# One sequential kernel, re-timed by hand: expert work two slots earlier, and stages re-filled on five queues

## What is computed

```
for each of 16 chunks of 128 tokens, four heads:
    out   = (silu(q W0^T) * (q W2^T)) W1^T            # with the weights so far
    dW    = gradients from k, v with those weights     # dW0, dW1, dW2
    M     = dW + mean(momentum) * M
    X     = M / |M|;  5 times:  A = X X^T;  B = b A + c A A;  X = a X + B X
    W     = renorm(W + X)                              # used by the next chunk
attention: windows of 128 + 128 keys, softmax, 2 heads of 128
y      = x + (norm(out) * scale + attention) Wo
experts: scores = sigmoid(xn gate^T); 2 of 4 groups of 8 experts, then 8 experts a token
         h = relu(x_lat w1_e)^2 * weight;  routed = sum_e(h w2_e) fc2
shared : relu(xn up)^2 down                            # 512 wide
result = y + routed + shared
```

## Time and profile before

| | us |
|---|---|
| median of 3 runs | 764.44 (762.72 to 765.95) |
| the profiled execution | 764.44 |
| its span, first to last instruction | 762.5 |
| PE busy | 662.8 (87% of the span) |
| DVE busy | 545.3 (72%) |
| ACT busy | 408.4 (54%) |
| POOL busy | 235.5 (31%) |

### The profile page before, as it was taken

How to read it: one execution, slowest core, us unless ns; L and a number is a source line. 1 busy time by engine, 2 the same in 40 slices (tenths; PEclk the granted TensorE clock), 3 DMA queues, 4 the chain that set the end, 5 groups by cost and what they waited for, 6 DMA issues and landing times.

```text
span 762.5 us, 22396 instructions
## 1 busy us (share of the span) xinstructions
PE 662.8 (87%) x8887; PEld 549.6 (72%) x8887; DVE 545.3 (72%) x1893; ACT 408.4 (54%) x1061; POOL 235.5 (31%) x299
## 2 busy tenths in 40 slices
PE   4788787999998889999999999999999999996865
PEld 2667565777786677878788788877878778784654
DVE  6865887685564496777868778687777867758673
ACT  3576352543543547656465564755657476462541
POOL 2422122146762131312213131132221313117761
PEclk9799989999999899999999999999999999999997
DMA  8300000041102024453552545444454544101221
GB/s 276 123 2 2 1 3 1 2 174 38 46 20 78 30 63 141 135 181 120 155 180 93 182 129 172 154 140 161 130 178 140 159 135 142 36 5 32 61 80 52
DMA packets 40152, 75.38 MB, mean 99 GB/s; under 512 B 9712, under 2 KB 24432, under 8 KB 40048
## 3 DMA queue, kind: packets, MB, share of 16 engines
q1 hardware_dynamic: 36224, 68.08, 28.0%
q0 software_dynamic: 2048, 4.33, 1.9%
q10 hardware_dynamic: 1776, 1.54, 0.6%
HBM read 64.73 MB, written 9.20 MB: 97 GB/s over the span
## 4 chain that ended last, share of the span: by engine, by line
PE 52%; DVE 28%; ACT 7%; issue 7%; POOL 3%; DMA 2%; SPq 0%; DVEq 0%; ACTq 0%; POOLq 0%
PE CC L828 16%; PE YB L828 12%; PE HB L828 10%; PE M L828 8%; DVE hb L1698 4%; DVE Am L1408 2%; POOL xsrc L447 2%; ACT hb L562 2%; DVE Mp L1414 2%; PE CC L921 1%; ACT XT L562 1%; DVE comb L1517 1%; PE M L1010 1%; PE CC L960 1%; POOL r L422 1%
## 5 line engine op out<-in xcount | busy, mean ns | idle before, releaser
L422 POOL TENSOR_TENSOR r<-r,half 128x3 f32<-128x3 f32 (+1 forms) x78 | 88.6, 1142 | 206.8 <-DVE r L1285 112.9
L1408 DVE TENSOR_TENSOR Am<-CC,shifts 128x192 f32<-128x192 f32 x150 | 47.6, 352 | 80.9 <-PE CC L828 80.7
L562 ACT ACTIVATE XT<-CC 128x256 f32<-128x256 f32 x150 | 50.9, 382 | 85.0 <-PE CC L922 84.6
L828 PE MATMUL YB<-e_s,hb 128*128 128x128 f32 x560 | 78.3, 283 | 5.9 <-DVE hb L1698 5.9
L562 ACT ACTIVATE hb<-HB 128x512 f32<-128x512 f32 x86 | 51.3, 597 | 54.6 <-PE HB L828 53.4
L828 PE MATMUL HB<-xsT,e_s 128*128 128x128 f32 x560 | 78.8, 284 | 1.7 <-issue 1.7
L828 PEld LDWEIGHTS YB<-e_s,hb 128*128 128x128 f32 x560 | 68.6, 191 | 16.1 <-DVE hb L1698 9.5
L1698 DVE TENSOR_TENSOR hb<-hb,cwb 128x512 f32<-128x512 f32 x70 | 76.1, 1087 | 0.0
L828 PEld LDWEIGHTS HB<-xsT,e_s 128*128 128x128 f32 x560 | 68.3, 192 | 4.6 <-issue 1.8
L828 PE MATMUL CC<-X,Mp 64*64 64x64 f32 x1800 | 57.0, 234 | 16.5 <-DVE Mp L1414 16.5
L828 PE MATMUL CC<-Am 64*64 64x64 f32 x1800 | 55.9, 233 | 14.0 <-DVE Am L1408 13.9
(11 more groups left out here) (229 smaller groups left out, 1505.9 us busy)
## 6 DMA issues: line engine op xcount, KB each, us to landing
e_s<-in_e1T SPq DMA_DIRECT2D x35, 512.0 KB, 4.6
e_s<-in_e2T SPq DMA_DIRECT2D x35, 512.0 KB, 5.6
cwb<-tile_weights SPq DMA_DIRECT2D x35, 512.0 KB, 3.7
sorted_rows<-e_s SPq DMA_DIRECT2D x5, 476.0 KB, 10.2
xs<-sorted_rows SPq DMA_DIRECT2D x35, 68.0 KB, 5.3
sorted_out<-yo SPq DMA_DIRECT2D x35, 64.0 KB, 2.9
out<-xnT_all SPq DMA_DIRECT2D x8, 256.0 KB, 2.1
x_all<-in_x SPq DMA_DIRECT2D x1, 1408.0 KB, 14.8
```

The source lines that it names most:

```text
L422: return pool.tensor_tensor(dst, src, expo[:, 0:n], ALU.pow)
L562: return nc.scalar.activation(out_, in_, func, **kw)
L828: return pe.matmul(out_, lhsT, rhs, start=start, stop=stop)
L1408: nc.vector.tensor_tensor(Am[g][:, :, :], PROD[g], shifts[:, it, :].unsqueeze(1).to_broadcast([P, 3, HD]), ALU.add)\
```

## The change

Five things are altered; no instruction's shape is, and nothing is computed otherwise.

1. The tables: routed units start at slot 35, where it was 37, and the shared units move with them by two or three slots.
2. The routing steps on DVE: one after each group's part of each stage (in step 1 only after group 1), where they stood after three of four stages in ones, twos and threes. PE's `prefixes` stands at stage 11, before at 14.
3. POOL's transfers: 3, 4, 5, 5, 3 behind the five places, before 4, 5, 6, 6, 3; scatters start in step 2 behind "key norm" (before: behind "row norm"), gathers in step 13 behind "output norm" (before: "row norm").
4. In each step: unit 3's second product and its first product change places (PE stages 5 and 6, before 7 and 5); on ACT relu and square of it stand at 6 and 7; on DVE `h_weight(3)` at 9 (before 7), `att_out` at 17 (before 18), `h_weight(5)` at 18 (before: in the tail, ahead of `renorm`); on PE `h_slot(7)` stands ahead of both `turn_w`, before between them.
5. The last two steps: the sixth pair's `last_sum`, `last_turn`, `last_yT`, `last_fc2` go into step 14's tail, ahead of `turn_w`, and in the closing step the rest stand elsewhere.

```diff
-FIRST = 4 * PER + 5
-SHARED = [2 * PER + 1, 2 * PER + 2, 2 * PER + 3, 2 * PER + 5, 2 * PER + 6, 2 * PER + 7,
-          3 * PER, 3 * PER + 1, 3 * PER + 3, 3 * PER + 4, 3 * PER + 6, 3 * PER + 7, 4 * PER, 4 * PER + 1,
-          13 * PER + 3, 13 * PER + 5]
+FIRST = 4 * PER + 3
+SHARED = [PER + 6, PER + 7, 2 * PER, 2 * PER + 1, 2 * PER + 3, 2 * PER + 4, 2 * PER + 5, 2 * PER + 7,
+          3 * PER, 3 * PER + 2, 3 * PER + 3, 3 * PER + 5, 3 * PER + 6, 4 * PER, 13 * PER + 1, 13 * PER + 3]
...
-                move(i, "key side", 4)
+                move(i, "key side", 3)
...
-            SCATTER_AT, GATHER_AT = (2, 4), (13, 4)
+            SCATTER_AT, GATHER_AT = (2, 3), (13, 2)
...
-                        4: [lambda: prep_qk(m)], 5: [lambda: prep_v(m), lambda: h_slot(i, 3)],
-                        7: [lambda: prep_small(m), lambda: y_slot(i, 3)],
+                        4: [lambda: prep_qk(m)], 5: [lambda: prep_v(m), lambda: y_slot(i, 3)], 6: [lambda: h_first(i, 3)],
+                        7: [lambda: prep_small(m), lambda: h_sq(i, 3)],
...
                 if i == LAST - 1:
                     last_yT(4)
+                    last_yT(5)
...
                     att_turn(i)
-                    last_turn(5)
                     q_out(i)
-                    last_fc2(5)
                     att_scores(i, True)
                     last_turn(6)
+                    last_fc2(6)
                     att_turn_p(i, True)
-                    last_fc2(6)
                     att_pv(i)
                     last_turn(7)
+                    last_fc2(7)
                     turn_comb(i)
-                    last_fc2(7)
                     out_wo(i)
...
-                        5: [lambda: h_slot(i, 3)], 7: [lambda: y_slot(i, 3)], 8: [lambda: prep_mom(m)],
+                        5: [lambda: y_slot(i, 3)], 6: [lambda: h_slot(i, 3)], 8: [lambda: prep_mom(m)],
...
                 y_slot(i, 7)
+                h_slot(i, 7)
+                if i == LAST - 1:
+                    last_turn(5)
+                    last_fc2(5)
                 turn_w(m, 0)
-                h_slot(i, 7)
                 turn_w(m, 1)
...
-                        7: [lambda: prep_silu_v(m), lambda: h_weight(i, 3)], 8: [lambda: prep_ss8(m), lambda: shared_add(i, 3)],
-                        9: [lambda: prep_mean(m)],
+                        7: [lambda: prep_silu_v(m)], 8: [lambda: prep_ss8(m)],
+                        9: [lambda: h_weight(i, 3), lambda: prep_mean(m)],
...
-                        18: [lambda: att_out(i)]}
+                        17: [lambda: att_out(i)], 18: [lambda: h_weight(i, 5)]}
...
+                        if routing and (i, st) >= (SORT_STEP, 1) and (g or i > SORT_STEP):
+                            routing.pop(0)()
...
-                    if st % 4 != 1 and (i, st) > (SORT_STEP, 1):
-                        for n in range(1 if i == SORT_STEP else 3 if st % 4 == 3 else 2):
-                            if routing:
-                                routing.pop(0)()
...
-                h_weight(i, 5)
                 renorm(m)
                 w_bd(m)
+                if i == LAST - 1:
+                    last_sum(5)
+                    last_out(4)
                 total(i)
```

More of the change, by code:

```diff
@@ L501, in body @@
                     rms_pow(i)
+                    while moved:
+                        moved.pop(0)()
                     return
@@ L506, in body @@
                 k_u(i, 1)
-                move(i, "key side", 4)
+                move(i, "key side", 3)
                 for g in range(G):
                     ss_pow(i, g)
-                move(i, "momentum norm", 5)
-                fill = {3: [lambda: rms_pow(i), lambda: move(i, "output norm", 6)],
-                        9: [lambda: prep_n8(m), lambda: move(i, "key norm", 6)],
+                move(i, "momentum norm", 4)
+                fill = {3: [lambda: rms_pow(i), lambda: move(i, "output norm", 5)],
+                        9: [lambda: prep_n8(m), lambda: move(i, "key norm", 5)],
                         16: [lambda: window(m)], 17: [lambda: prep_kl(m)]}
@@ L522, in body @@
                     row_pow(m, g)
-                move(i, "row norm", 2 * NT if i == LAST - 1 else 3)
+                move(i, "row norm", 3)
             def move(i, behind, count):
@@ L736, in body @@
                     gate_sig(i)
-                    last_yT(5)
+                    q_out(i)
                     act.preload_act_table_set("natural_log_exp_and_others")
-                    q_out(i)
                     last_yT(6)
@@ L1165, in body @@
                 if i == SORT_STEP:
-                    fill[14] = [prefixes] + fill[14]
+                    fill[11] = [prefixes] + fill[11]
                 if i == LAST - 1:
@@ L1735, in body @@
                     q_ms(i)
-                    last_out(5)
                     att_mask(i)
                     att_max(i)
-                    q_norm(i)
                     last_sum(7)
                     last_out(6)
+                    q_norm(i)
                     att_out(i)
@@ L1751, in body @@
                 grad(i)
-                shared_add(i, 0)
                 sum_copy(i, 0)
@@ L1756, in body @@
                 x_first(i)
+                shared_add(i, 0)
                 fill = {0: [lambda: shared_add(i, 1), lambda: att_scale(i)], 2: [lambda: h_weight(i, 1), lambda: shared_add(i, 2)],
                         3: [lambda: q_ms(i)], 5: [lambda: q_norm(i), lambda: prep_silu_qk(m)],
-                        6: [lambda: h_weight(i, 2), lambda: prep_z(m)],
-                        7: [lambda: prep_silu_v(m), lambda: h_weight(i, 3)], 8: [lambda: prep_ss8(m), lambda: shared_add(i, 3)],
-                        9: [lambda: prep_mean(m)],
+                        6: [lambda: h_weight(i, 2), lambda: prep_z(m), lambda: shared_add(i, 3)],
+                        7: [lambda: prep_silu_v(m)], 8: [lambda: prep_ss8(m)],
+                        9: [lambda: h_weight(i, 3), lambda: prep_mean(m)],
                         10: [lambda: lr_a(m), lambda: prep_qkn(m), lambda: shared_add(i, 4)],
@@ L1797, in body @@
                 if i == LAST - 1:
-                    last_out(4)
-                    last_sum(5)
+                    last_out(5)
             dve.wait_ge(e_init, 2)
```

## The result

The changed kernel took **770.09** in the median (767.25 to 771.63), the kernel before, timed beside it, 765.61: ratio **1.006**, interval 1.0046 to 1.0075. It is slower. The forecast of 761.7 was wrong in sign; the time lies above the range. A few executions ran in a far slower state (one of the kernel before took 1494.83), and all ratios here, and the median of experiment 5, leave them out.

The account below looks back on a forecast made before the run. It took PE, busy 87% of the span, and the waits between engines in one chain of steps as the bound. Its terms by step summed to -2.7 from 764.44, giving 761.7, range 755.2 to 769.0.

Parts of the forecast that it names:

- Step 2: Second step: step 3's old pattern plus a second product, the tail and scatters make it 53.5, +2.2 (0 to +4).
- Step 3: Third step: 4.0 less fill at 0.64 a microsecond, plus 0.6 for the tail and stages: -2.0 (-3.4 to -0.5).
- Step 4: Fourth step: waits and half-clock stretches go because other work holds those places; 46.9, -7.0 (-8 to -3).
- step 1: First step after step 0: routing between Am and Mp and two shared units lengthen it by 3.0 (+1 to +5).
- Steps 5 to 12: The eight steady steps: +0.6 each from the step's end and stages 5 to 9, +4.8 (-2 to +13).
- stages 5 to 9: Within steps 5 to 12: unit 3's new order covers PE's wait but delays X and XT; +0.2 a step (-0.3 to +0.5).
- the prediction's sentence by the rule: End of steps 5 to 12: comb ends 0.28 after the first or second kl, tail about +0.1 or +0.7.
- Step 13: Thirteenth step: 4.5 less fill gives -1.8, `att_out` +0.4, together -1.4.
- closing step: Last stretch: DVE's 3.49 wait goes, `turn_w` 2.2 later, att_pv up to 1.9 earlier less 0.4; -1.5 (-3 to +1).
- Neutral steps: Rival: steps 5 to 12 stay at 46.5, steps 1 to 4 and 13 lose 0.3 less each; 755.4, chance 0.25.
- The clock: Rival: in step 4 TensorE's lower clock or late rows keep 3.5 of the 7.0; 765.2, chance 0.17.
- Slower: Rival: comb waits for all POOL's kl and vl, 0.9 more a step in steps 2 to 13; 772.5, chance 0.13.

Follow-up runs that it names:

- experiment 5: The changed kernel with `att_out` back at stage 18 and `h_weight(5)` back in the tail ahead of `renorm`: median 767.1, ratio 1.0009 to the kernel before.
- experiment 1: The changed kernel with `shared_add(i, 0)` put back ahead of `sum_copy`: 766.9, ratio 0.9998 to the kernel before.
- experiment 2: The kernel before with only `shared_add(i, 0)` moved behind `x_first`: 771.25, ratio 1.0059 to the kernel before.
- experiment 4: The changed kernel with step 2's routing and scatters in the old rhythm and POOL's transfers in the old numbers: 768.89, ratio 1.0034 to the kernel before.
- run 9: Run 8 with the sixth pair's work and the closing step's order also put back, gathers staying early: 761.05, ratio 0.9917 to the kernel before.
- run 8: The changed kernel with `shared_add(i, 0)` back ahead of `sum_copy` and `h_slot(7)` back between the turns of W: 762.55, ratio 0.9937 to the kernel before.
- 11: Run 9 with `last_fc2(6)` moved ahead of `att_turn_p` in the closing step: 760.45, ratio 0.9942 to the kernel before.

## Why the prediction was wrong, point by point

**Step 2, the step that failed.** The prediction gave step 2 "step 3's old pattern plus a second product" and took step 3's length for it. It read the table of slots and not where DVE's `shared_add(i, 0)` had gone, past `x_first`; the prediction has no sentence on that move. It held step 3's pattern to be unchanged when the instruction that had let it run without a wait was moved in the same diff. The wait and the slow clock behind it are 4.0 in the profile and 4.8 by the ratios (experiment 1); the same move alone costs the kernel before 4.5 (experiment 2). The remaining 54.54 is 1.0 over the forecast 53.5, in the upper half of its bounds. Which term this 1.0 belongs to is open: for routing and scatters the prediction had +1.0, and undoing both gave back 0.6 (experiment 4). The other moved one, `shared_add(i, 3)`, was not tried in these steps.

**Step 3, -2.0 against +1.3.** Two mistakes. First, the boundary: in step 2 the time from the end of the last Mp to the end of `renorm` fell from 6.75 to 5.24, but from that Mp to the end of the next momentum it is 14.69 before and 14.93 after. So what step 2 seems to save at its end, step 3 pays at its start (its momentum ends at +9.69, before at +7.94); that PE's queue of shared products is the bound there is argued, not shown. Second, the fill: behind the momentum step 3 is only 0.4 shorter for two products less. Two products left its start (the first Am came 1.7 sooner after the momentum) and one left the second iteration (-1.6); the third changed by -0.7; but one came into the first iteration, which had none (+1.75), and one into the last, which had one (+1.7). Over steps 1 to 4 the forecast had -3.8. In run 9, which has neither the wait nor the new order of turns, they take 200.5, in the kernel before 200.4: what step 4 gives, steps 1 to 3 take. The fill of these four is 66.0 after and 61.5 before, for which 0.64 a microsecond would ask +2.9; the half-clock stretches that step 4 had before are in the same sum, so it neither bears the 0.64 out nor refutes it.

**Step 4 and step 1** came out as forecast: 46.5 where no half-clock stretch fell in (46.9 forecast), 47.85 with one; step 1 +2.7 for +3.0. That step 1 agrees to 0.3 is luck in part, for it took 46.95 to 49.05 in the profiles with the new table and 43.4 to 44.7 in those with the old. The reason for step 4, PE idling in a step with no excuse, was right too. The fault was to count it as a net gain of the table.

**Steps 5 to 12**, mis-sized by 4.0 in all. The parts, a step each: `att_out` +0.24 (forecast +1.0), `h_weight(5)` -0.39 and the order of the turns +0.34 (together forecast -0.6), stages 5 to 9 -0.12 (forecast +0.2). They sum to +0.07; measured +0.08 in most steps. For `att_out` comb's time was the smaller part: 0.57 and not 0.82. The larger was the update's start, which the prediction put at "some 0.8 later"; it had been held by comb before. For the turns the sign was wrong: the prediction named the lost cover of ACT's copies and then gave the reordering a gain. Comb ran from 456.04 to 456.61, beside the pair of kl's. The first kl took 0.62 and ended at 456.33, 0.28 before comb; the second took 0.80 and ended at 457.09. So comb waited for one kl and held up the other, as the prediction's sentence by the rule had it, and not for all three products. The Trainium skill ("SBUF — State Buffer", section "Who interferes with whom") states that such a pair of instructions contends for an exclusive lock; the trace agrees.

**Steps 13, 14 and closing.** Step 13 was as long as before, with 4.5 less fill (46.65 and 46.71). The -1.8 for it was too much by the prediction's own rows: 1.8 is what step 1 saves by having none of the 18.0. Whether the fill was worth nothing or the gathers that now start in step 13 (POOL busy 21.17 against 11.00) took it back was not tested. In the closing step DVE's wait of 3.49 went, as forecast, and `turn_w` came 3.2 after the second Wn against 1.1 before: 2.1, where 2.2 were forecast. The loss behind att_pv, put at 0.4, was 1.8, since `last_fc2(7)` ran at 1.2 GHz ahead of comb's turn.

**The rivals.** "Neutral steps" was right for steps 5 to 12, and only partly by its own reasons: comb was let in after the first kl and stages 5 to 9 gained, but the loss by the turns and the gain by `h_weight(5)`, 0.34 and 0.39, it did not name. "The clock" held 1.3 of step 4. "Slower" gave the sign by a mechanism that did not occur: comb never waited for all of POOL's products. The prediction would have called itself wrong if the steady steps moved by more than 1; they moved by 0.08, and it was wrong by a step that it counted once.

## What to carry to other kernels

When a diff changes a table and moves an instruction, run the new table through the new order: find every place where two users of one buffer follow each other, and ask what frees it between them. Fill that is moved is paid where it lands; only the waits that it covers are won. Undo the parts of a many-part change one at a time: here two parts won 0.34 percent by themselves, undoing two others took 1.2 percent off the changed kernel (from 1.006 to 0.9937), and the sum hid both.

## What the runs showed of the hardware

- DVE's hb (two inputs in SBUF) and POOL's vl, both times recorded 0.02 apart with vl first, took 1.08 and 1.58 in the changed kernel, and 1.55 and 0.61 in run 8. Step 11 of the changed kernel has it the other way as well, 1.54 and 0.61. One of the two runs at its own speed (1.07 and 0.61 where nothing is beside) and the other's time grows by 0.97 or 0.48; which one it is, the recorded starts don't tell.
- Each PE wait of 2.00 to 2.06 ahead of a shared product, in all seven profiles that have one, was followed by a granted clock of 1.2 GHz (from 133.1 in the changed kernel, from 183.2 and 237.9 in experiment 2), and the product took 2.6 to 3.6; in experiment 1, without the wait, the clock stayed and it took 1.89.
- The profiled last two steps of runs 9 and 11 differ by 5.4 (71.1 and 65.7) at one moved instruction; before the closing step their code is the same, and step 14 alone differs by 2.7, with TensorE at half clock for 6.8 from 700.5 in the one and not at all in the other. The medians differ by 0.6. A single profile can't settle an effect in a stretch that the clock slows.
